# Pooling one block ahead of its attention and seven inside it, in a fused pooling, attention and expert kernel

## What is computed

```python
def _L0_cond_ref(hidden, W1, b1, v, prompt_type_ids):
    attn_in = jnp.tanh(jnp.einsum('bsd,da->bsa', hidden, W1) + b1)
    scores = jnp.einsum('bsa,a->bs', attn_in, v)
    mask = jnp.where(pt == 0, prefix_m[None], jnp.where(pt == 1, postfix_m[None], cloze_m[None]))
    masked_scores = jnp.where(mask, scores[:, None, :], NEG_INF)
    p = jax.nn.softmax(masked_scores, axis=-1)
    cnt = jnp.sum(mask, axis=-1).astype(hidden.dtype)
    return jnp.einsum('bjl,bld->bjd', p, hidden) / cnt[..., None]
x = x + attention(pooled(x))        # 16 heads of 8, a rotary part shared by them, causal
h = x @ W[category] + b[category]   # one matrix per sequence, out of 64
x = x + experts(h)                  # sigmoid gate, 4 of 8 groups, 8 of 64 experts, and a shared one
```

## Time and profile before

| | us |
|---|---|
| median of 3 runs | 789.02 |
| lowest, highest | 788.45, 789.91 |
| the profiled execution | 791.17 |
| its span, first to last instruction | 789.0 |
| TensorE busy in it | 749.0 (95%) |
| VectorE, ScalarE, GpSimd busy | 558.3, 459.4, 424.5 |

### The profile page before, as it was taken

One profiled execution on the slowest core, in us unless ns is written; L12 is line 12 of the kernel. 1 busy time (PEld: TensorE's weight loads), 2 busy tenths in 40 slices (PEclk: granted clock), 3 DMA queues, 4 the chain that ended last, 5 costly groups with the idle time before them and its releaser, 6 DMA issues.

```text
span 789.0 us, 16047 instructions
## 1 busy us (share of the span) xinstructions
PE 749.0 (95%) x5766; PEld 580.4 (74%) x5766; DVE 558.3 (71%) x1147; ACT 459.4 (58%) x877; POOL 424.5 (54%) x348
## 2 busy tenths in 40 slices
PE   6787679999999999999999999999999999999997
PEld 5766557777778777777778777777778777787885
DVE  5851856597677885697668885688669866786664
ACT  3454267556765567556755567547755676555553
POOL 1355525465545565555546555556646654566665
PEclk9899879999999999999999999999999999999999
DMA  5245244543334435443344334343454335347441
GB/s 198 91 151 153 66 106 132 120 124 106 121 119 122 132 107 142 110 129 107 123 127 113 119 109 151 108 140 87 137 127 122 110 102 150 95 120 147 127 122 52
DMA packets 67903, 95.15 MB, mean 121 GB/s; under 512 B 7888, under 2 KB 26768, under 8 KB 67824
## 3 DMA queue, kind: packets, MB, share of 16 engines
q1 hardware_dynamic: 64368, 90.98, 41.0%
q10 hardware_dynamic: 3456, 3.15, 1.2%
HBM read 88.66 MB, written 4.98 MB: 119 GB/s over the span
## 4 chain that ended last, share of the span: by engine, by line
PE 78%; ACT 7%; DVE 5%; SPq 3%; DMA 3%; POOL 2%; issue 1%; POOLq 0%; ACTq 0%; DVEq 0%
PE G L880 22%; PE Y L880 21%; PE U L880 21%; PE A L880 11%; ACT s_t L362 2%; ACT hid_hi L490 2%; POOL hid_lo L574 1%; ACT L478 1%; ACT L362 1%; SPq L287 1%; SPq L281 1%; PE A L942 1%; DMA k_blk<-in_x_feat 1%; POOL wu_lo L548 1%; DVE act_w L851 1%
## 5 line engine op out<-in xcount | busy, mean ns | idle before, releaser
L574 POOL TENSOR_TENSOR hid_lo<-hid,hid_hi 128x512 fp32r<-128x512 f32 (+1 forms) x264 | 341.6, 1294 | 306.2 <-ACT hid_hi L490 305.3
L851 DVE TENSOR_TENSOR act_w<-G,cwb 128x512 f32<-128x512 f32 x248 | 170.6, 688 | 104.9 <-ACT G L478 98.4
L478 ACT ACTIVATE G<-G 128x512 f32<-128x512 f32 x248 | 144.3, 582 | 159.5 <-PE G L880 156.7
L490 ACT CAST hid_hi<-hid 128x512 fp32r<-128x512 f32 (+1 forms) x264 | 162.5, 616 | 60.7 <-DVE hid L863 60.0
L863 DVE TENSOR_TENSOR hid<-act_w,U 128x512 f32<-128x512 f32 (+1 forms) x256 | 175.8, 687 | 23.7 <-PE Y L880 2.0
L880 PE MATMUL G<-c_hi,wg_hi 128*128 128x512 f32 x248 | 114.8, 463 | 0.0
L880 PE MATMUL Y<-hid_hi,wd_hi 128*128 128x512 f32 (+1 forms) x264 | 106.8, 405 | 4.5 <-POOL hid_lo L574 4.5
L880 PE MATMUL Y<-hid_lo,wd_hi 128*128 128x512 f32 (+1 forms) x264 | 104.4, 395 | 0.0
L880 PE MATMUL Y<-hid_hi,wd_lo 128*128 128x512 f32 (+1 forms) x264 | 104.2, 395 | 0.0
L880 PE MATMUL U<-c_hi,wu_hi 128*128 128x512 f32 x248 | 99.0, 399 | 0.0
L880 PE MATMUL G<-c_hi,wg_lo 128*128 128x512 f32 x248 | 98.6, 398 | 0.0
(11 more groups left out here) (188 smaller groups left out, 952.8 us busy)
## 6 DMA issues: line engine op xcount, KB each, us to landing
cwb<-cw_scratch SPq DMA_DIRECT2D x256, 256.0 KB, 3.7
k_blk<-in_cond_w SPq DMA_DIRECT2D x128, 64.0 KB
xf<-in_x_feat SPq DMA_DIRECT2D x9, 256.0 KB, 4.2
cwb<-in_we_gate SPq DMA_DIRECT2D x8, 256.0 KB, 5.6
cwb<-in_we_up SPq DMA_DIRECT2D x8, 256.0 KB, 3.7
cwb<-in_we_down SPq DMA_DIRECT2D x8, 256.0 KB, 3.3
out_feat<-y ACTq DMA_DIRECT2D x8, 256.0 KB, 2.3
pooled_scratch<-s_t SPq DMA_DIRECT2D x7, 256.0 KB, 3.4
```

The lines of the kernel that those rows point to most:

```text
L478: nc.scalar.activation(gate_bank(p)[:, :], gate_bank(p)[:, :], ACT.Silu).then_inc(S["silu_done"], 1)
L490: nc.scalar.copy(hid_hi[0:n, p % NH, :], hid[0:n, p % NH, :]).then_inc(S["hi_ready"], 1)
L574: nc.gpsimd.tensor_sub(hid_lo[0:n, p % NH, :], hid[0:n, p % NH, :], hid_hi[0:n, p % NH, :].bitcast(F32)).then_inc(S["lo_ready"], 1)
L851: nc.vector.tensor_mul(act_w[:, p % NH, :], gate_bank(p)[:, :], cwb[:, p % NCW, :])\
```

## The change

What it does:

- Only block 0 is pooled before its attention. The others form two groups, blocks 1 to 3 and 4 to 7 (`POOLED`); their hidden products, scores, softmax, spreading and products stand between steps of block 0's attention, and the last three products after its routing.
- The mask is one comparison of a constant tile (sign of l - j) with a number per sequence. Its result times -1e30 is added to the scores. Counts are made of differences.
- The token-major input is loaded (`x_tok`) instead of being transposed by TensorE.
- The raw expert weights are loaded into the space of the remainders (`wg_raw` begins where `wg_lo` does), so no load waits for a split. Sixteen splits after the first go by steps, 8 of 25 go into units 0 to 7, and GpSimd waits for the routing weights (`cw_ready`) before it does splits 9 to 16. Units wait for the split of their four.
- TensorE's first matmul waits for two loads instead of six; a table load of ScalarE comes at the start; pooled blocks are stored from ScalarE's queue; the first category matrices go to `cwb`'s space; fewer warm-up matmuls; block 1's `first_products` and rotation come after block 0's routing.

The diff, cut to its core:

```diff
+        with ExitStack() as early:
+            def sb_early(name, shape):
+                return early.enter_context(nc.sbuf_tensor(name, shape, F32))
+
+            wg_raw, wu_raw = sb_early("wg_raw", [P, UNITS, P]), sb_early("wu_raw", [P, NPAIR, P])
+            wd_raw = sb_early("wd_raw", [P, UNITS, D])
+            x_early = sb_early("x_early", [P, 6, TOK])
+            spread_p = sb_early("spread_p", [P, 2, TOK])
+        wg_lo, wu_lo = sb("wg_lo", [P, UNITS, P], F32R), sb("wu_lo", [P, NPAIR, P], F32R)
...
+        POOLED = [(0, 1), (1, 4), (4, 8)]
+        BEFORE_UNITS = 17
+        WARM = {0: 4, 9: 6, 12: 2, 13: 2, 14: 2, 15: 2, 16: 2, 17: 2, 20: 2, 21: 20}
...
@@ sync
+            sp.dma_start(c[:, :], consts).then_inc(S["consts_in"], 16)
+            sp.dma_start(w[:, :], weights).then_inc(S["consts_in"], 16)
+            sp.dma_start(xf_in[0], x_feat[:, bass.ts(0, TOK)]).then_inc(S["x_in0"], 16)
+            sp.dma_start(pt_i, prompt).then_inc(S["prompt_in"], 16)
+            sp.dma_start(xt_in[0].rearrange("p (t d) -> p t d", d=D), x_tok[:, 0:TILES, :]).then_inc(S["xt_in0"], 16)
...
@@ scalar
+            def pooled_out(i):
+
+                act.wait_ge(S["pooled_ps"], i + 1)
...
+                nc.scalar.copy(pooled[i], Y[:, :]).then_inc(S["pooled_ready"], 1)
+                act.wait_ge(S["pooled_ready"], i + 1)
+                act.dma_start(h_dram[:, bass.ts(i, TOK)], pooled[i]).then_inc(S[f"h_stored{i}"], 16)
...
             for p in range(UNITS):
                 attention_step(p, 0)
-                if p == ROUND:
+                if p == 4:
+                    pool_hidden(2)
+                elif p == 8:
+                    pool_exp(1)
+                elif p == 10:
+                    pool_exp(2)
...
+                elif 12 <= p < 17:
+                    split(p - 10)
+                elif p == 17:
+                    pooled_out(1)
...
+                elif p == ROUND:
                     round_input(0, 0)
-                for i in SPLITS.get(p, ()):
-                    split(i)
+                    pooled_out(3)
+                    pooled_out(4)
+                elif 23 <= p < 31:
+                    split(p - 14)
+            for i in range(5, NBLK):
+                pooled_out(i)
...
+                if not prev and BEFORE_UNITS + p <= NSPLIT:
+                    split(BEFORE_UNITS + p)
@@ gpsimd
             for p in range(UNITS):
...
                 attention_step(p, 0)
-                for i in SPLITS.get(p, ()):
-                    split(i)
+                if 12 <= p < 19:
+                    split(p - 10)
+            pool.wait_ge(S["cw_ready"], 1)
+            for i in range(9, 12):
+                split(i)
             rope_add(1)
+            for i in range(12, BEFORE_UNITS):
+                split(i)
...
+                if not prev and BEFORE_UNITS + p <= NSPLIT:
+                    split(BEFORE_UNITS + p)
@@ vector
+            def select(first, last):
+
+                n = TILES * (last - first)
+                return nc.vector.tensor_tensor(
+                    sel[:, TILES * first:TILES * last, :], C["side"].unsqueeze(1).to_broadcast([P, n, SEQ]),
+                    target[:, TILES * first:TILES * last].unsqueeze(2).to_broadcast([P, n, SEQ]), ALU.is_equal)
...
+                if p == 4:
+                    pool_scores(1)
+                elif p == 9:
+                    pool_scores(2)
+                    pool_weights(1)
+                elif p == 16:
+                    spread(1)
+                    spread(2)
+                elif p == 18:
+                    pool_weights(2)
+                elif p == 20:
+                    spread(3)
+                    spread(4)
+            spread(5)
...
             rest_of_input(0, 0)
+            spread(6)
+            rotate(1)
+            spread(7)
...
@@ tensor
+            first_products(0)
+            pool_scores(1)
+            pool_hidden(2)
             for p in range(STEPS):
+                if p == CWT:
+                    warm(8)
                 attention_step(p, 0)
+                if p == 7:
+                    pool_scores(2)
...
+                elif p in (17, 18):
+                    pool_out(p - 16)
+                elif p == 21:
+                    pool_out(3)
+                    pool_out(4)
+                if p >= 9:
+                    warm(WARM.get(p, 0))
+            pool_out(5)
+            first_products(1)
+            pool_out(6)
+            pool_out(7)
```

More of the change, by code:

```diff
@@ L453, in _ @@
[L453 to L467 removed]
+            pool_exp(0)
@@ L510, in unit @@
                     act.dma_start(out[:, bass.ds(b * TOK - TOK, TOK)], y[:, :]).then_inc(S["y_free"], 16)
+                if not prev and BEFORE_UNITS + p <= NSPLIT:
+                    split(BEFORE_UNITS + p)
+                if p == 0 and not prev:
+                    for i in range(5, NBLK):
+                        act.wait_ge(S[f"h_stored{i}"], 16)
                 if p == X2_MOVED:
@@ new lines, in spread @@
+            def spread(i):
+                if i >= 2:
+                    dve.wait_ge(S["pooled_ps"], i - 1)
+                for s in range(SPT):
+                    rows = slice(SEQ * s, SEQ * s + SEQ)
+                    last = nc.vector.transpose(pool_pt[i % 2][rows, :, s, :], pool_p[rows, bass.ts(i, TILES), :])
+                last.then_inc(S["pool_spread"], 1)
+            nc.vector.memset(small[:, :], 0.0).then_inc(S["blank"], 1)
+            dve.sem_inc(S["weighted"], NPAIR)
+            setup(nc.vector.memset(vrep[:, :, :], 0.0))
@@ L1033, in _ @@
+                last.then_inc(S["pooled_ps"], 1)
+            warm(4)
             pool_hidden(0)
-            for i in range(HALF):
-                turn(i)
+            pe.wait_ge(S["vrep_ready"], 1)
+            pool_scores(0)
             pool_hidden(1)
-            pe.wait_ge(S["dve_chain"], CHAIN_SETUP)
-            pool_scores(0)
-            for i in range(HALF, HALF + 2):
-                turn(i)
+            pool_out(0)
+            pe.wait_ge(S["setup"], 2)
+            first_products(0)
```

435 lines of the change are left out of this document (207 added, 228 removed).

## The result

| | before | after |
|---|---|---|
| median, us (runs) | 789.46 (4) | 755.36 (4) |
| lowest, highest | 788.45, 790.12 | 753.82, 756.97 |
| profiled execution, its span | 791.17, 789.0 | 754.20, 752.4 |

The ratio is 0.9559, with an interval of 0.9538 to 0.9580. The forecast was 757.8, its range 749 to 766.

The account below looks back on a forecast made before the run. TensorE was taken as full from 112.5 us on, so only the start of block 0's unit 9 counted: 28.0 + 2.3 + 6.0 - 5.1 = 31.2 us off the 789.0 us span, forecast 757.8 us, range 749 to 766.

Parts of the forecast that it names:

- The frame: Asks when block 0's expert unit 9 starts, 131.90 us before, with the way there split at F, R and T.
- F: Mark at block 0's first product: 43.00 us before, 15.0 forecast.
- R: Mark at block 0's first routing instruction: 83.48 us before.
- T: Mark where block 0's routing weights are ready: 97.4 us before, 61.1 forecast.
- term 2: Block 0's attention, F to R, with seven blocks' pooling inside: 40.5 becomes 38.2 us, gain 2.3; bounds gain 6, loss 6.
- Term 1: The opening, 0 to F: earlier first matmul and only one block's pooling on the path, gain 28.0 us, bounds 24 and 30.
- The third case: Rival, chance 0.20: woven vector instructions wait for GpSimd's, then ScalarE and TensorE wait; term 2 becomes 5 lost, 765 us.
- Term 3: Block 0's routing, R to T: no GpSimd splits beside VectorE's small instructions, 14 becoming 8 us, gain 6.0.
- Term 4: Hand-over, T to unit 9: ScalarE and GpSimd end a new wait in units 4 to 9; 34.5 becomes 39.6, loss 5.1.
- other edits at nothing: Mask by comparison, raw weights in their own space, table load at the start and other addresses: counted as no change.
- other addresses: The changed places of tensors in memory, counted at nothing.

Follow-up runs that it names:

- second execution of the changed kernel: The changed kernel run and profiled again with nothing edited; 756.48 us, 0.9566 of before.
- the last kernel: Changed kernel with both parities' rounded inputs low, the rearranged hand-over to the units, and idle matmuls fitted to the gaps; 748.59 us, 0.9472 of before.
- warm opening: Changed kernel with 14 idle matmuls before block 0's pooled product and 3 after it; 755.40 us, 0.9552 of before.
- the run with the softmax first: Changed kernel with the other seven blocks' pooling up to the softmax put ahead of block 0's pooled product again, on all engines; 764.66 us, 0.9681 of before.

## Why the prediction held, and which steps failed

**The frame** (ask when unit 9 starts, and split the way at F, R and T) held: the four terms sum to 31.65 us, 31.2 forecast. That they agree so closely is in part luck. In the second execution of the changed kernel the same four gave 27.5, since term 2 turned into a loss, and the total was saved there by the 3.8 us behind unit 9 that nobody had forecast.

**Term 1**, 28.0 forecast, 25.95 measured. The mechanism is right. Two terms of its sum were too small. One is the weights' landing, 1.0 us: 4.4 forecast, 5.40 measured, 4.7 to 5.1 in most other executions. The other is the pooled product, 0.7 us: the row of 1.35 us stands in a stretch of before (35 to 40 us) with a granted clock of 0.52, so it was no price of the upper level either; there the product takes 1.06, and here, after 3.29 us of standing, it took 2.08. With idle matmuls in that gap F came at 16.09, and at 15.61 in the last kernel, where the weights were there at 4.69.

**Term 2**, 2.3 forecast, 3.4 and, in the other execution, a loss of 0.8 measured (F to T is 48.72, less 7.40 of routing, is 41.3). Both lie within the bounds of 6 either way, but for a reason to which the prediction gave no price: the clock. With the first products at the upper level the score tiles start 9.5 us behind F (warm opening), and 10.4 or 10.5 in both executions of the changed kernel; behind them the second lost its 4.3 us. The pieces of the sum missed, too, and in part made up for each other: the rope mask came 10.1 us behind F, not 8.1, and the copies of the probabilities stood 1.45 us apart, not 1.7. The third case ("woven work is late") did not come: the woven softmax is hidden, as the run with the softmax first shows.

**Term 3**, 6.0 forecast, 6.5 measured, and shown by putting splits back (14.6 us again). The Trainium skill's page "SBUF — State Buffer", section "Who interferes with whom", has VectorE's instructions with two SBUF inputs wait for GpSimd's that read SBUF, for their whole length; the 1.34 beside 0.29 us of one instruction agrees. The same rule, taken against the change, would have made term 2 lose up to 5.2. It didn't: the woven subtractions and multiplications took 0.56 and 0.69 us, none of them lengthened, since GpSimd ran nothing at the moments at which they came.

**Term 4**, 5.1 forecast, 4.2 measured; first SiLU at 73.98 (75 forecast), unit 9 at 100.25 (101 forecast), and the wait is ended by the two engines named. The order shown in the hand-over was the cause.

**The step that failed** is the clause in "other edits at nothing": "other addresses". The units were called untouched, and stretches after 110 us that differ were named as what would be wrong. They do differ: 4.95 us, of which addresses alone give 4.4. It didn't spoil the total since it is a seventh of it. Of the other misses only term 1's (2.05 us) goes the other way; terms 2, 3 and 4 each came out better than forecast, by 2.5 together. Set against the medians: 31.2 us forecast, 34.1 measured.

The pitch would account for more than arrived: 1107 matmuls in even blocks by 0.7 ns and 1188 in odd ones by 5.0 are 6.7 us, of which 4.95 came; with all streamed operands low, 2295 by some 4.7 are 10.8, and 6.5 came. Where the rest goes is shown for one block above: not into the attention's matmuls, but mostly to down products beside the routing.

## What to carry to other kernels

Work that only later blocks need can be woven into the first block's attention at almost no cost: the softmax of seven blocks took 12 us ahead of it, and no more than 0.8 us inside it, by the fastest execution of the changed kernel. It should not stand beside VectorE's chain of small instructions if it runs on GpSimd: there seven splits made the routing 7 us longer. When TensorE's work moves, its gaps move, and idle matmuls must be put into the new ones, as many as fit. Too few cost 4 to 5 us at the lower clock from F to T, too many 3.6 us there by overshoot (47.1 us instead of 43.5). An allocation that changes is an edit: where the streamed operands of the units' matmuls lie is worth 2% of their pitch.

## What had not been expected of the hardware

- **The pitch of 512-column matmuls depends on where the streamed operands lie in the partition**: 233 ns with all of them at 169 to 210 thousand bytes, 228 to 229 with all below 76 thousand, 231.6 with the input moved and the hidden tile not. A matmul whose own operand lies low among others that lie high gains 2 to 2.5 ns only. The Trainium skill's page "TensorE: Matmul & The Clock Gate", section "Wait — 56ns, not 53.3ns?", gives 215.7 ns for back-to-back matmuls of that width at the upper level; the traces here don't reach it: the lowest mean is 228.1, with the other engines at work.
- **The lower clock falls in different places from one execution to the next** and does so for the same program: at 15 to 25 us in one, at 25 to 35 and 40 to 45 us in the other, each time beside gaps of 2.4 to 3.3 us of TensorE. Not every such gap is followed by it: in the first, TensorE stood 2.29 us at 35 us and the clock stayed at 1.00. The granted clock and the durations don't always agree: in the second of these it reads 1.00 at 15 to 20 us, where the first product took 2.05 us. There the duration was believed.
